# Low parts of the gated rows formed by TensorE and copied by ScalarE, with one buffer for the mixing sums

## What is computed

```
xn = layernorm(x)
w  = sigmoid(relu(xn @ W1 + b1) @ W2 + b2)        # one gate per node
num[row] += (xn * w)[col]; den[row] += w[col]      # over the 200,000 edges
x  = x + num / den + mix(xn)                       # mix: out = xn @ (k^T v / N) + xn, by heads
x  = x + experts(layernorm(x))
```

## Time and profile before

| | |
|---|---|
| median of three executions | 1694.67 us (1690.87 to 1698.68) |
| the profiled execution | 1685.33 us |
| its span | 1683.5 us |
| engine busy, share of the span | PE 84%, PEld 79%, DVE 80%, ACT 47%, POOL 37% |
| granted TensorE clock, mean | 0.932 |
| the stretch of the change | 344.65 us (first gated row) to 456.25 us (sort ended) |

### The profile page before, as it was taken

The page is one execution under the profiler, slowest core; times in us unless marked ns, Lnnn a source line. Parts: engine busy times, 40 slices in busy tenths (PEclk is TensorE's granted clock), DMA queues, the critical chain, the costliest instruction groups (busy, mean ns, idle before and its releaser), DMA issues.

```text
span 1683.5 us, 39514 instructions
## 1 busy us (share of the span) xinstructions
PE 1417.3 (84%) x12059; PEld 1323.5 (79%) x12059; DVE 1349.0 (80%) x3945; ACT 797.1 (47%) x1958; POOL 616.9 (37%) x617
## 2 busy tenths in 40 slices
PE   0137898666389999999999999999999679999997
PEld 0136787556379999999999999999999669999996
DVE  8999999999968878788787887877878566676665
ACT  1113555255435555555554555555445345555553
POOL 1563767563312222222222222222222333335565
PEclk9758999667789999999999999999999889999999
DMA  7100000023351011110111101111111155444553
GB/s 184 19 0 1 1 1 1 1 87 109 113 170 39 35 47 38 43 45 34 47 38 42 45 34 47 38 38 47 38 47 38 68 186 135 139 123 78 85 95 54
DMA packets 71141, 102.26 MB, mean 61 GB/s; under 512 B 13790, under 2 KB 53579, under 8 KB 70823
## 3 DMA queue, kind: packets, MB, share of 16 engines
q1 hardware_dynamic: 50294, 56.99, 12.1%
q0 software_dynamic: 20352, 43.71, 9.4%
q10 hardware_dynamic: 432, 0.79, 0.1%
HBM read 45.34 MB, written 57.47 MB: 61 GB/s over the span
## 4 chain that ended last, share of the span: by engine, by line
PE 67%; DVE 23%; issue 4%; ACT 2%; DMA 2%; DVEq 1%; POOL 0%; SPq 0%; POOLq 0%; another core or an unknown queue 0%; ACTq 0%
PE turned L1394 18%; PE front L1394 17%; DVE sort_mem L1696 16%; PE turned L1376 10%; PE turned L1533 5%; PE front L1533 5%; PE front L1553 5%; DVE sort_mem L1704 2%; PE front L1423 1%; PE turned L1333 1%; PE turned L1526 1%; ACT a_ring L1130 1%; PE front L1416 1%; DVE acc_mem L2094 1%; DMA gath_mem<-in_dst 1%
## 5 line engine op out<-in xcount | busy, mean ns | idle before, releaser
L1793 DVE TENSOR_TENSOR sort_mem<-lane_bf,sort_mem 128x512 bf16<-128x512 bf16 x1372 | 518.9, 420 | 150.5 <-PE turned L1376 137.1
L1130 ACT ACTIVATE a_ring<-turned 128x384 fp32r<-128x384 f32 (+1 forms) x686 | 373.5, 545 | 417.7 <-PE turned L1376 409.7
L1394 PE MATMUL turned<-y_all,a_ring 128*128 128x258 f32 x2450 | 387.8, 296 | 8.8 <-ACT a_ring L1130 8.8
L1394 PE MATMUL front<-y_all,a_ring 128*128 128x258 f32 x2352 | 377.1, 297 | 8.2 <-ACT a_ring L1130 8.1
L1696 DVE TENSOR_TENSOR sort_mem<-sort_mem 128x320 f32<-128x320 f32 (+2 forms) x568 | 329.3, 642 | 3.0
L1394 PEld LDWEIGHTS turned<-y_all,a_ring 128*128 128x128 f32 x2450 | 318.6, 191 | 13.0 <-issue 11.4
L1394 PEld LDWEIGHTS front<-y_all,a_ring 128*128 128x128 f32 x2352 | 306.1, 190 | 12.5 <-ACT a_ring L1130 11.2
L1376 PE MATMUL turned<-sort_mem 128*128 128x128 bf16 (+1 forms) x2695 | 259.9, 217 | 4.4 <-DVE sort_mem L1793 2.2
L963 POOL DMA_INDIRECT out_rows<-base x108 | 144.2, 1335 | 160.5 <-DVE base L2105 92.5
L1376 PEld LDWEIGHTS turned<-sort_mem 128*128 128x128 bf16 x2695 | 139.7, 98 | 41.1 <-DVE sort_mem L1793 9.8
L1333 PE MATMUL turned<-ident,sort_mem 128*128 128x128 f32 x286 | 57.0, 360 | 112.1 <-DVE sort_mem L1696 111.3
(11 more groups left out here) (258 smaller groups left out, 1968.6 us busy)
## 6 DMA issues: line engine op xcount, KB each, us to landing
base<-token_lists SPq DMA_DIRECT2D x54, 258.0 KB
base<-token_lists SPq DMA_DIRECT2D x54, 130.0 KB
gated_rows<-tab_mem SPq DMA_DIRECT2D x49, 128.5 KB, 3.0
late_mem<-mixed_rows SPq DMA_DIRECT2D x49, 128.0 KB, 2.0
mixed_rows<-base SPq DMA_DIRECT2D x12, 512.0 KB, 3.3
feat_mem<-in_L_ffn_expert_w SPq DMA_DIRECT2D x18, 256.0 KB
base<-in_x SPq DMA_DIRECT2D x1, 3136.0 KB
base<-in_x SPq DMA_DIRECT2D x1, 2352.0 KB
```

Of the source, the lines that this page charges most:

```text
L1130: nc.scalar.activation(a_ring[:, k % 2, :, :].rearrange("p s n -> p (s n)")[:, 0:width], ps_a[k % 2][:, 0:width], ACT.Copy).then_inc(S["a_ ...
L1394: last = nc.tensor.matmul(ps_agg[odd], a_ring[:, k % 2, n, :], y_part(t, part), start=(t == 0 and part == 0), stop=(t == BLOCKS - 1 and pa ...
L1793: nc.vector.tensor_tensor(hot[:, k % 2, 0:pairs, :, :], lane_bf[:, :, :].unsqueeze(1).broadcast_to([P, pairs, P, 2]), edges.unsqueeze(2).b ...
```

## The change

The low part moves from GpSimd to TensorE and ScalarE. For block t TensorE forms identity x row + (-identity) x high part in PSUM (`low_part(t)`), and ScalarE copies the result to `y_all` (`keep_low(t)`), behind `gated(t + 1)`. GpSimd's subtractions are gone. The negated identity is a matrix in `a_ring`, made once by ScalarE. The two places for the low parts are banks 2 and 3 of `front`, which held the second buffer of the mixing sums; the mixing sums now have one buffer, banks 0 and 1, so that `mix(batch)` waits for the copy of batch-1. On TensorE the table MIX_AT is gone: `mix(0)` stands before `low_part(0)`, and `mix(b + 1)` behind `low_part(4b + 5)`. All of it still stands between the same two turns as the gated rows of its blocks.

```diff
-MIX_AT = {(16, 6): (0, 1), (17, 16): (1, 4), (17, 6): (4, 6), (18, 17): (6, 10), (18, 6): (10, MIX_BATCHES)}
...
-        ps_mix = [front[:, s * MIX_TILES * DIM:(s + 1) * MIX_TILES * DIM].rearrange("p (t n) -> p t n", t=MIX_TILES) for s in range(2)]
+        ps_mix = front[:, 0:MIX_TILES * DIM].rearrange("p (t n) -> p t n", t=MIX_TILES)
...
+        ps_low = [bank(2 + n)[:, 0:PART] for n in range(2)]
+        minus_ident = a_ring[:, 0, 0, :]
...
-            for t in range(BLOCKS):
-                pool.wait_ge(S["hi_ready"], t + 1)
-                if t:
-                    pool.wait_ge(S["split_ready"], t)
-                nc.gpsimd.tensor_tensor(y_part(t, 1), y_out[:, t % Y_SLOTS, :], y_part(t, 0).bitcast(F32), ALU.subtract).then_inc(S["split_ready"], 1)
...
-                nc.scalar.activation(base[:, at:to, :], ps_mix[batch % 2][:, 0:to - at, :], ACT.Copy).then_inc(S["mix_done"], 1)
+                nc.scalar.activation(base[:, at:to, :], ps_mix[:, 0:to - at, :], ACT.Copy).then_inc(S["mix_done"], 1)
+
+
+            def keep_low(t):
+                act.wait_ge(S["low_ps"], t + 1)
+                nc.scalar.activation(y_part(t, 1), ps_low[t % 2], ACT.Copy).then_inc(S["split_ready"], 1)
 
 
             def gated_and_mixed(t, last):
                 gated(t)
+                if t:
+                    keep_low(t - 1)
...
+                        if t == 0:
+                            nc.scalar.activation(minus_ident, ident[:, :], ACT.Copy, scale=-1.0).then_inc(S["minus_ready"], 1)
                         gated_and_mixed(t, MIX_LAST)
+            keep_low(BLOCKS - 1)
...
-                if batch >= 2:
-                    pe.wait_ge(S["mix_done"], batch - 1)
+                if batch:
+                    pe.wait_ge(S["mix_done"], batch)
...
+            def low_part(t):
+                if t == 0:
+                    pe.wait_ge(S["minus_ready"], 1)
+                pe.wait_ge(S["hi_ready"], t + 1)
+                if t > 1:
+                    pe.wait_ge(S["split_ready"], t - 1)
+                nc.tensor.matmul(ps_low[t % 2], ident[:, :], y_out[:, t % Y_SLOTS, :], start=True, stop=False)
+                nc.tensor.matmul(ps_low[t % 2], minus_ident, y_part(t, 0), start=False, stop=True).then_inc(S["low_ps"], 1)
...
-                    for batch in range(*MIX_AT.get((level, bit), (0, 0))):
-                        mix(batch)
+                    for t in range(*GATED_AT.get((level, bit), (0, 0))):
+                        if t == 0:
+                            mix(0)
+                        low_part(t)
+                        if t >= MIX_LAG and (t - MIX_LAG) % MIX_TILES == 0:
+                            mix((t - MIX_LAG) // MIX_TILES + 1)
+            mix(MIX_BATCHES - 1)
...
+            pe.wait_ge(S["split_ready"], BLOCKS)
```

More of the change, by code:

```diff
@@ L502, in gps_layer @@
             mix_ps mix_done mixed_stored mixed_loaded
-            dst_lane_ready slot_step hi_ready split_ready kept_stored below_ps
+            dst_lane_ready slot_step minus_ready low_ps hi_ready split_ready kept_stored below_ps
             count_ready key_at_ready key_held window_in unkeyed_ready found_ready lanes_ready valid_ready lanes_f_ready edges_turned
@@ L1316, in mix @@
                     pe.wait_ge(S["kv_final"], 1)
-                if batch >= 2:
-                    pe.wait_ge(S["mix_done"], batch - 1)
+                if batch:
+                    pe.wait_ge(S["mix_done"], batch)
                 for t in range(batch * MIX_TILES, min(batch * MIX_TILES + MIX_TILES, BLOCKS)):
-                    sums = ps_mix[batch % 2][:, t % MIX_TILES, :]
+                    sums = ps_mix[:, t % MIX_TILES, :]
                     nc.tensor.matmul(sums, ident[:, :], base[:, t, :], start=True, stop=False)
```

## The result

| | before | after |
|---|---|---|
| median of four executions each, us | 1695.97 (1690.87 to 1698.68) | 1723.01 (1714.62 to 1727.52) |
| profiled execution, us | 1685.33, span 1683.5 | 1720.35, span 1718.6 |
| TensorE starts turn (17, 16), us | 359.56 | 374.7 (forecast 368.6) |
| turn (17, 6) | 385.59 | 404.9 (397.0) |
| turn (18, 17) | 403.82 | 428.7 (417.1) |

After takes 1.0173 times the time of before, interval 1.0137 to 1.0208: 1.7% slower. That is the forecast (1715, range 1701 to 1732). The profile shows nearly all of it ahead of the sort's end: +30.2 us there, and 1718.6 - 486.4 = 1232.2 us behind it against 1683.5 - 456.25 = 1227.3.

The account below looks back on a forecast made before the run. VectorE was taken to bound the five sort stages with gated rows. The walk's +14 us, 2 for releases and waits and 4 for the clock made +20: 1715 on the median of 1694.67, range 1701 to 1732 (8 in 10).

Parts of the forecast that it names:

- Relief of VectorE: In the five sort stages with gated rows, VectorE's compare steps get faster without GpSimd's subtractions: 18 us on offer.
- The rival in which VectorE gets no faster: Subtraction gone, compare steps no faster: last stage keeps 17.1 us, +2.4, 1717; counted within the forecast, no chance of its own.
- Costs of one low part: Per block, a copy holds ScalarE 0.30 us; the products take TensorE 0.57 us at the upper clock, 1.11 at the lower.
- The round: Per four blocks, single buffering makes TensorE (4.3 us) and ScalarE (4.0 us) take turns: 8.3 us.
- The walk: Through five stages at the upper clock: turns late by 8.2, 11.4, 13.3, 17.6 us; sort's end 470.4 against 456.25, +14.
- `kv` later than 350.99: Ahead of the first turn, batch 0 was taken to wait for `kv` as before and end at 357.6; nothing added.
- batches at the lower clock: One to two mixing batches on TensorE at the lower clock, 3.1 us more each: 4 us added.
- releases and double waits: More of these in each round than counted, 0.2 us for ten rounds: 2 us added.
- The gain comes through: Rival: ScalarE never waits at a low part, its work sets the pace, sort ends at 438: -18 us, 1677; 6%.
- Break-even: Rival: waits half as costly, last turn some 3 us late, cancelled by the last stage's gain: 1695; 9%.
- The clock stays low: Rival: TensorE's rounds take 12.2 us, 39 us on top of 14: 1748; half slow, 1729 to 1733; 12%.

Follow-up runs that it names:

- zero_low: Kernel before with GpSimd's subtraction replaced by a memset of the low part, low parts left out of the result: 1637.34 us, ratio 0.9875.
- before_again: Kernel before, unchanged, profiled once more on another chip: 1658.17 us, sort's end 459.4.
- two_lows: Kernel after with low-part products for blocks 0 and 1 alone, ScalarE still making all 49 copies: 1667.81 us, ratio 1.0057 to the kernel before.
- spread: Kernel after with one block of mixing behind each low part instead of four behind every fourth: 1657.42 us, ratio 0.9999 to the kernel before.
- twice: Kernel after with each low part's identity product done twice, the first overwritten: 1680.11 us, ratio 1.0135 to the kernel before.
- one_buffer: Kernel before with one buffer for the mixing sums and nothing else changed: 1659.81 us against 1657.87, ratio 1.0012.
- late_mix: spread with mixing five blocks behind the low parts, none ahead of the first turn, gated rows 8, 12, 8, 14, 7 per stage: 1647.22 us, ratio 0.9932 to before.

## Why the prediction was right

**Relief of VectorE: 18 us forecast, 20.5 measured.** *zero_low* is 20.5 us faster; its sort ends at 441.1, 18.3 us ahead of before_again's 459.4. The rival in which VectorE gets no faster has fallen.

The prediction held the rows against the rule of the Trainium skill (SBUF — State Buffer, "SBUF: two separate sides") that the loser of the shared ports is fully blocked, and read them as less than the rule's full size, since 18 us are less than the 43.4 us of subtractions. That reading was wrong, and the single instructions in the trace of before show why. The trace agrees with the rule at its full size. The 859 ns are a mean of two kinds: of the 68 steps of 128x512, 43 take 676 to 692 ns, as alone, and 25 take 1016 to 1223. Each of the 25 began while a subtraction was already running. The 886 ns of a subtraction are in part waiting too: 48 of the 49 began while a VectorE operation was running, and 46 of these end 0.50 to 0.60 us after the end of that operation. One pair of each kind (ns min/median/max, start in us); in the first the subtraction was there first, in the second the step:

```profile
L849 POOL TENSOR_TENSOR y_all<-tab_mem,y_all x1: 906/906/906, 377.1 to 377.1; 128x258 fp32r<-128x258 f32 x1
L1696 DVE TENSOR_TENSOR sort_mem<-sort_mem x1: 1124/1124/1124, 377.4 to 377.4; 128x512 f32<-128x512 f32 x1
...
L1696 DVE TENSOR_TENSOR sort_mem<-sort_mem x1: 676/676/676, 370.9 to 370.9; 128x512 f32<-128x512 f32 x1
L849 POOL TENSOR_TENSOR y_all<-tab_mem,y_all x1: 1157/1157/1157, 371.0 to 371.0; 128x258 fp32r<-128x258 f32 x1
```

So a subtraction keeps VectorE out for some 0.5 us, and only where it came first. That was so for 25 steps of 128x512 and 10 of 128x320, and VectorE's steps of the two shapes took 17.3 us more in all than alone. Priced so, the rule gives the 18 us of the rows, and no lower forecast. The busy time of a blocked engine is no measure of what the other one gives up.

The same section says that a VectorE operation with two SBUF inputs meets the lock only against a GpSimd operation that reads SBUF. With that the runs agree: beside 49 memsets, which read nothing, a 128x512 step takes 684 ns, and 687 in the kernel after, where GpSimd does nothing at all.

**Costs of one low part: right.** The copies, ns min/median/max, against 382 for the nearest form in the earlier trace rows:

```profile
L1066 ACT ACTIVATE y_all<-front x49: 367/368/388, 363.3 to 484.3; 128x258 fp32r<-128x258 f32 x49
```

The operation behind one starts after 0.27 us (446.73 to 447.00); 0.30 was forecast. ScalarE's round without waits for low parts, 6.3 in the forecast from the earlier trace rows, is 6.1 in *two_lows*. TensorE's low part takes 0.56 us at the upper clock (449.46 to 450.02 in its timeline; 0.57 was forecast).

**The round: right, and shown to be the cause.** 8.34 us in the trace, 8.3 forecast. With the product of the low part taken out it falls to 6.1, with the batch cut into blocks to 6.7, with one product added it rises to 8.9. Order and not work makes it: *spread* has the same instructions and loses nothing against the kernel before.

**The walk: +16 us late at the sort's end against its 470.4, by three terms.**

| term | forecast | in the trace |
|---|---|---|
| `kv` later than 350.99 | 0 | 5.0 |
| batches at the lower clock | 4 | 9.2 |
| releases and double waits, the remainder | 2 | 1.8 |

The clock term was mis-sized. It rested on one to two batches at 3.1 us each. Ahead of the last turn the trace has six that begin at the lower clock, behind low parts with gaps between them, and regain the upper one before their end. Two of the six:

```profile
413.54 1.22 PE L1325 MATMUL front<-base,ident 128*128 128x256 f32 x2
415.41 1.06 PE L1325 MATMUL front<-base,ident 128*128 128x256 f32 x2
416.92 0.60 PE L1325 MATMUL front<-base,ident 128*128 128x256 f32 x2
...
423.39 1.13 PE L1325 MATMUL front<-base,ident 128*128 128x256 f32 x2 [0.37 <-ACT base L1061]
```

L1325 takes 1.22 and 1.06 us in the first two blocks and 0.60 in the third. Batches 1, 4, 5, 6, 9 and 10 take 4.77, 5.19, 5.12, 5.26, 5.26 and 5.27 us against 3.61 of batches 2, 3, 7 and 8 (0.88 a block in the earlier trace rows): 9.2 us more. Batch 0 was at the lower clock in the forecast too, and batch 11 (4.1 us) lies in the last stage, where VectorE bounds. *twice* bears on the term from the other side: without the lower clock in these batches, and with 0.5 to 0.6 us a round added, it takes 5.4 us less between `kv` and the last turn. Ten rounds add 6 us if all of them lie on the path and none if none does, which puts the clock's part between 5.4 and 11.4 us, an estimate. The remainder of 1.8 us holds the low part of block 42, 0.56 us, which the walk left out ahead of turn (18, 6).

The `kv` term was not forecast at all: the walk took "as before" for a time that is 351.0 or 355.8 in one and the same kernel. In the kernel after all that lies between `kv` and the first turn is on the path, so that the 5.0 us count in full. In the kernel before the delay costs less and by another way, VectorE's wait at turn (16, 6), and before_again's sort ended 3.2 us later (459.4 against 456.25). The profiled pair has the short time before and the long one after, and overstates the change. With the long one in both it would be 486.4 - 459.4 = 27.0 us, an estimate, since the two profiles come from two chips. The medians are 27.0 us apart.

**The sum.** +20 was forecast and +27 measured. Of the 7 us between them the clock is 5 (9.2 for 4), and `kv` 1.8 (5.0 less 3.2) where both kernels have it late; both parts are estimates from one profile each. All the errors of the sum point the same way, so none hid another, and the range was wide enough for them. One reading of the earlier trace rows is off without a consequence: ScalarE's least idle time in a stage is 5.1 us (15.50 less 10.38), not 4.7.

**The rivals.** *The gain comes through* fell: ScalarE does wait at the low parts. The view of waits, 356 to 487 us (who, for whom: us in total, times, longest us):

```profile
ACT y_all L1066 <- PE front L1339: 34.4, 11, 15.0
```

Without the longest, whose low part stands behind `kv` and batch 0, these are ten waits of 1.9 us, once per batch, as forecast. *Break-even* fell by the first turn, 15 us late. *The clock stays low* fell too: no round within a stage took 12.2 us; the slow ones took 9.9 and 10.0 (from batch 5 at 413.5 to batch 6 at 423.4, and from batch 9 at 454.2 to batch 10 at 464.2), since TensorE regained the clock in mid-batch. That the second buffer's loss alone costs the time fell with *one_buffer*. No run keeps both buffers beside the low parts, so what a second buffer would save there is not shown.

**What stays open.** Why GpSimd's small operation gets in between two VectorE steps in some executions and is kept out for 6.1 or 7.6 us in others (last section) was not tried. *late_mix* changed three things at once (the lag, the blocks per stage, no mixing ahead of the first turn), and no run parts them.

## What to carry to other kernels

Work that is moved to another engine joins a program order. Ask what stands ahead of it there: a product of 0.57 us became a wait of 2 us per round because it stood behind a batch of 3.5 us that itself waited for the consumer of the product. Two engines that each need 6 us for a round take 8.3 when a single buffer lets only one of them work at a time, and cutting the batch into the grain of the small work brings that back without a buffer. Before you price a contention, part the durations of single instructions: a busy time can be the engine's own wait. Price the relief (here 20 us) and the lateness at each hand-over apart; the second decides, and it adds up from stage to stage.

## What the runs showed that was not expected

- **TensorE's clock within a round.** Two low parts and gaps precede each batch. The busy times by stretch, columns as above:

```profile
441.57:445.85 4.28, 2.48 (x12) 1.47 (x10) 4.28 (x11) 3.90 (x11) 0.00 (x0) 1.00 0.18 62
446.00:454.00 8.00, 6.38 (x36) 5.12 (x36) 7.66 (x16) 5.79 (x17) 0.00 (x0) 1.00 0.40 134
449.90:454.18 4.28, 2.48 (x11) 1.47 (x9) 3.75 (x8) 3.90 (x11) 0.00 (x0) 1.00 0.25 83
454.20:457.60 3.40, 3.40 (x12) 3.04 (x13) 0.00 (x0) 2.20 (x7) 0.00 (x0) 0.51 0.58 190
```

  TensorE was busy 2.48 of 4.28 us ahead of the batch at 445.85, which ran at the upper clock, and again 2.48 of 4.28 ahead of the one at 454.18, which began at the lower one. What TensorE did just before a batch doesn't tell which batch is hit. Evenly spread work kept the clock: 1.00 in *spread* from 370.5 to 459.2 us, and in *late_mix* in all four stretches above. More work did too: *twice*, with 49 products thrown away, had 0.99 over the whole stretch and was no slower than the kernel after for them.
- **A small GpSimd operation with three durations.** The operation on 128x49 took 0.54 us in three of ten profiles (before, *twice*, *late_mix*), 6.1 in five and 7.64 in two (after, *zero_low*), in kernels of either kind. The long ones are waits for VectorE. In before_again it spans 333.34 to 339.48, and VectorE's steps meanwhile take what they take alone:

```profile
L1696 DVE TENSOR_TENSOR sort_mem<-sort_mem x12: 479/580/682, 333.3 to 338.9; 128x512 f32<-128x512 f32 x6, 128x320 f32<-128x320 f32 x6
```

  Each of these steps starts some 0.08 us before the one ahead of it shows its end. The operation ends beside the first step that starts behind such an end, at 339.39. In all seven long cases it is so, after 11 or 15 steps in such a row, and *one_buffer* has a subtraction of the same kind:

```profile
L849 POOL TENSOR_TENSOR y_all<-tab_mem,y_all x1: 8838/8838/8838, 378.1 to 378.1; 128x258 fp32r<-128x258 f32 x1
```

  VectorE lost nothing meanwhile, and GpSimd stood still. In the cases of 0.54 us it got in although the steps overlapped in the same way.
- **GpSimd's memset costs VectorE nothing that shows**: 684 ns a step beside memsets against 687 with GpSimd idle. It is itself 313 ns where the subtraction, its waits included, was 886.
